# A short setup for a token tower: counts from two 16-way one-hots, and attention logits in unsplit f32 by quarters of the array

## The reference

```
h = take(weight.T, x)                       # 64 x 128 tokens, 64 features
n = layernorm(h)
q, k, v = n @ Wq, n @ Wk, n @ Wv            # 8 heads of 64
a = sigmoid(8 * einsum('bifh,bjfh->bijh', q, k))
h = h + relu(einsum('bijh,bjfh->bifh', a, v) @ Wo)
n = layernorm(h)
h = h + sum over the two best of 6 experts of gate * mlp3(n)
```

## Time and profile before

| | us |
|---|---|
| median of 3 runs | 335.9 |
| lowest, highest | 335.36, 340.27 |
| the profiled execution | 338.1 |
| its span, first to last instruction | 336.3 |
| start of the first unit (end of the setup) | 63.05 |

### The profile page before, as it was taken

One profiled execution on the slowest core, in us unless ns is written; L12 is line 12 of the kernel. 1 busy time (PEld: TensorE's weight loads), 2 busy tenths in 40 slices (PEclk: granted clock), 3 DMA queues, 4 the chain that ended last, 5 costly groups with the idle time before them and its releaser, 6 DMA issues.

```text
span 336.3 us, 4648 instructions
## 1 busy us (share of the span) xinstructions
PE 241.6 (72%) x1636; PEld 130.7 (39%) x1636; DVE 211.6 (63%) x493; ACT 129.1 (38%) x242; POOL 140.4 (42%) x180
## 2 busy tenths in 40 slices
PE   0797663556699699880853457297979899898984
PEld 0555563555556276440323445131424243232221
DVE  4336799756457567452164766867888877946432
ACT  1125437335455355340111402424453455454540
POOL 3000224188987978975021274271536240410110
PEclk9999977585779789996795755877999799999999
DMA  8218300047777667667000003782475556848741
GB/s 173 41 52 122 79 2 0 0 129 206 202 207 193 176 184 204 176 179 219 0 0 2 1 2 77 158 175 59 88 178 135 132 111 128 189 99 179 175 91 31
DMA packets 32263, 38.28 MB, mean 114 GB/s; under 512 B 21936, under 2 KB 23024, under 8 KB 32240
## 3 DMA queue, kind: packets, MB, share of 16 engines
q1 hardware_dynamic: 20240, 20.36, 28.0%
q0 software_dynamic: 10336, 17.05, 18.7%
q10 hardware_dynamic: 1664, 0.58, 0.8%
HBM read 18.30 MB, written 2.83 MB: 63 GB/s over the span
## 4 chain that ended last, share of the span: by engine, by line
PE 37%; DVE 23%; POOL 13%; DMA 12%; issue 6%; ACT 6%; SPq 2%; ACTq 0%; POOLq 0%; DVEq 0%
POOL G L231 12%; DMA G<-Gs 7%; PE PS L688 6%; PE PS L813 5%; PE PS L784 5%; PE PS L800 4%; PE PS L726 4%; DVE OHt L884 3%; PE PS L670 3%; ACT H L502 3%; DVE lead L1076 2%; DVE ex L1078 2%; DMA xb<-ids_scratch 2%; DMA wo_s<-wo 2%; DVE AH L926 2%
## 5 line engine op out<-in xcount | busy, mean ns | idle before, releaser
L231 POOL DMA_DIRECT2D G<-Gs x128 | 76.4, 605 | 19.1 <-DVE Gs L993 10.4
L670 PE MATMUL PS<-AH,BD 128*128 128x256 f32 x256 | 41.0, 326 | 19.5 <-ACT Gs L487 9.9
L688 PE MATMUL PS<-G,cnt 128*64 128x512 f32 x128 | 36.2, 692 | 15.4 <-DMA G<-Gs 15.4
L670 PEld LDWEIGHTS PS<-AH,BD 128*128 128x128 f32 x256 | 38.6, 231 | 22.1 <-DVE BD L946 11.3
L1055 DVE SCALAR_TENSOR_TENSOR H2g<-PS,nb_s,WB 128x1024 f32<-128x1024 f32 x24 | 30.7, 1280 | 14.7 <-PE PS L800 14.7
L993 DVE COPY Gs<-PS 128x512 f32<-128x512 f32 x32 | 21.1, 687 | 28.2 <-DMA G<-Gs 24.8
L502 ACT ACTIVATE H<-PS,b_s 128x512 f32<-128x512 f32 x48 | 30.3, 681 | 19.4 <-PE PS L784 19.4
L800 PE MATMUL PS<-H,W2s 64*64 64x512 f32 x192 | 27.9, 653 | 8.3 <-ACT H L502 8.2
L487 ACT ACTIVATE Gs<-PS 128x512 f32<-128x512 f32 x32 | 18.0, 596 | 40.9 <-DMA G<-Gs 32.6
L961 DVE SCALAR_TENSOR_TENSOR Htab<-PS,table 128x128 f32<-128x128 f32 x64 | 16.8, 382 | 22.8 <-PE PS L699 22.7
L784 PE MATMUL PS<-X,W1s 64*128 64x512 f32 x96 | 29.4, 692 | 0.7 <-ACT H L502 0.7
(11 more groups left out here) (117 smaller groups left out, 405.2 us busy)
## 6 DMA issues: line engine op xcount, KB each, us to landing
G<-Gs POOLq DMA_DIRECT2D x128, 128.0 KB, 3.7
WB<-gate_scratch SPq DMA_DIRECT2D x16, 768.0 KB, 8.8
xb<-ids_scratch SPq DMA_DIRECT2D x8, 256.0 KB, 6.5
h_out<-Y SPq DMA_DIRECT2D x8, 256.0 KB, 6.8
VOr<-vo_scratch SPq DMA_DIRECT2D x2, 512.0 KB, 7.0
GG<-gate_scratch SPq DMA_DIRECT2D x64, 12.0 KB
vo_scratch<-VOs SPq DMA_DIRECT2D x1, 512.0 KB, 3.9
cst<-consts SPq DMA_DIRECT2D x1, 313.0 KB, 4.6
```

The source lines that it names most:

```text
L231: eng.dma_start(G2[half % G2_RING][first:first + 4 * (CG - 1) + 1:4, :, :], Gs[n % GS_RING][:, m, :]).then_inc(done[n % GS_RING], 16)
L670: ins = pe.matmul(o, BD[n % BD_RING][:, part, gl].rearrange("p c f -> p (c f)"), AH[:, r * UG + gl, :], start=(part == 0), stop=(part == 1))
L688: ins = pe.matmul(PS[u * NB:(u + 1) * NB, B_O + m % 2, :], cnt[:, k, :], G2[(2 * fg + k) % G2_RING][:, f:f + 2, :].rearrange("p f a -> p ( ...
```

## The change

The setup is written anew; the stages of the table and the tokens keep their instructions and their order.

- **Counts.** The eight bits of an id are parted into two sets of four (masks 0x4E and 0xB1). DVE masks the ids twice and compares each against 16 constants for all 64 rows at once (`OHa`, `OHb`: 128 x 1024 each). 64 matmuls of 16 x 16 give the counts, after logits step 1. DVE copies them to `cnt_l` after step 5, and two DMAs on SyncE's queue (SP) bring them to `cnt`'s layout.
- **Logits.** `TS` holds unsplit f32, 64 columns to a group, the same in both halves of the partitions; ACT copies banks 0 and 2, DVE banks 1 and 3. `NDhi` and `NDlo` are gone. A step is eight f32 matmuls on quarters of the array.
- **Order.** PE transposes the table ahead of the `WVO` products; `VOp` is cut after steps 0 and 2.

```diff
-VO_AT = 3
-OH_EARLY = 8
-OB = 4
+VO_AT = 0
+NC = 16
+BH = NB // 2
...
-        TS = sb("TS", [P, NG, 2, CG, HEADS], F32R, setup)
-        OHt = sb("OHt", [P, 2, OB, NV], BF16, setup)
+        TS = sb("TS", [P, NG, CG, HEADS], F32, setup)
+        xa, xc_ = sb("xa", [P, NB], I32, setup), sb("xc_", [P, NB], I32, setup)
+        OHa, OHb = sb("OHa", [P, NB, NC], BF16, setup), sb("OHb", [P, NB, NC], BF16, setup)
+        cnt_l = sb("cnt_l", [D, NC, BH], F32, setup)
...
@@ send_unit, and contract(0) alike
-                eng.wait_ge(cnt_sb, 1)
+                eng.wait_ge(cnt_ld, 32)
...
@@ sync, ahead of the first two x_load
+            sp.wait_ge(cnt_sb, 2)
+            for u in range(2):
+                sp.dma_start(cnt[:, :, u * BH:(u + 1) * BH],
+                             cnt_l[32 * u:32 * u + NC].rearrange("a (n k) b -> a n k b", k=VK)).then_inc(cnt_ld, 16)
...
@@ scalar
-            for b in range(4):
+            for b in (0, 2):
                 act.wait_ge(t_ps, b + 1)
-                act.activation(head_pair(TS[:, :, 0], b),
+                act.activation(head_pair(TS[:], b),
...
@@ tensor
+            def counts():
+
+                pe.wait_ge(oh_ready, 2)
+                for b in range(BH):
+                    for u in range(2):
+                        ins = pe.matmul(PS[32 * u:32 * u + NC, 5, b * NC:(b + 1) * NC], OHa[:, u * BH + b, :],
+                                        OHb[:, u * BH + b, :], start=True, stop=True)
+                ins.then_inc(cnt_ps, 1)
...
-            pe.wait_ge(nd_lo, 1)
-            pe.wait_ge(t_dup, 2)
+            pe.wait_ge(t_act, 2)
+            pe.wait_ge(t_dve, 2)
             for t in range(8):
                 if t >= 2:
                     pe.wait_ge(as_ready, t - 1)
-                for j in range(4):
-                    o = PS[:, 2 * (t % 2) + j // 2, (j % 2) * NV:(j % 2 + 1) * NV]
-                    w = TS[:, 4 * t + j].rearrange("p u c h -> p (u c h)")
-                    pe.matmul(o, w, NDhi[:], start=True, stop=False)
-                    ins = pe.matmul(o, w, NDlo[:], start=False, stop=True)
+                for j in (0, 2, 1, 3):
+                    rows = slice(D * (j // 2), D * (j // 2) + D)
+                    for v in range(2):
+                        ins = pe.matmul(PS[v * D:(v + 1) * D, 2 * (t % 2) + j // 2, (j % 2) * NV:(j % 2 + 1) * NV],
+                                        TS[rows, 4 * t + j].rearrange("p c h -> p (c h)"), nT[rows, :],
+                                        start=True, stop=True, skip_group_check=True)
                 ins.then_inc(lg_ps, 1)
-                if t >= 2:
-                    for a in one_hots_with(t - 2):
-                        count(a)
+                if t == 1:
+                    counts()
...
@@ vector
+            dve.tensor_scalar(xa[:], xt_i[:], A_BITS, None, ALU.bitwise_and).then_inc(x_bits, 1)
+            dve.tensor_scalar(xc_[:], xt_i[:], B_BITS, None, ALU.bitwise_and).then_inc(x_bits, 1)
+            for n, (oh, bits, at) in enumerate(((OHa, xa, C_CA), (OHb, xc_, C_CB))):
+                dve.wait_ge(x_bits, n + 1)
+                dve.tensor_tensor(oh[:], bits[:].unsqueeze(2).broadcast_to([P, NB, NC]),
+                                  cst[:, at:at + NC].unsqueeze(1).broadcast_to([P, NB, NC]), ALU.is_equal)\
+                   .then_inc(oh_ready, 1)
...
+            for b in (1, 3):
+                dve.wait_ge(t_ps, b + 1)
+                dve.tensor_copy(head_pair(TS[:], b),
+                                PS[:, T_BANKS[b], :].rearrange("p (h g c) -> p h g c", h=2, c=CG)).then_inc(t_dve, 1)
```

More of the change, by code:

```diff
@@ L64 @@
 H_RING = 5
-C_ID, C_IOTA, C_MASK, C_SEL, C_BM, C_TIE, C_ROW, C_END = 0, 128, 130, 138, 138 + 192, 334, 370, 370 + 256
+C_ID, C_IOTA, C_MASK, C_SEL, C_BM, C_TIE, C_CA, C_CB, C_END = (
+    0, 128, 130, 138, 138 + 192, 334, 370, 370 + NC, 370 + 2 * NC)
+A_BITS, B_BITS = 0x4E, 0xB1
 def home(r, m):
@@ L177, in build @@
         ld_r, ld_w1, ld_b, ld_w2, ld_w3 = (sem(n) for n in ("ld_r", "ld_w1", "ld_b", "ld_w2", "ld_w3"))
-        ln0, ln0_pool, const_ready, nT_ps, nT_sb, nd_hi, nd_lo, x_f = (sem(n) for n in (
-            "ln0", "ln0_pool", "const_ready", "nT_ps", "nT_sb", "nd_hi", "nd_lo", "x_f"))
+        ln0, ln0_pool, const_ready, nT_ps, nT_sb, x_bits = (sem(n) for n in (
+            "ln0", "ln0_pool", "const_ready", "nT_ps", "nT_sb", "x_bits"))
         ld_ids, ids_ok, ids_st = sem("ld_ids"), sem("ids_ok"), sem("ids_st")
-        k_ps, k_sb, t_ps, t_hi, t_lo, t_dup = (sem(n) for n in ("k_ps", "k_sb", "t_ps", "t_hi", "t_lo", "t_dup"))
+        k_ps, k_sb, t_ps, t_act, t_dve = (sem(n) for n in ("k_ps", "k_sb", "t_ps", "t_act", "t_dve"))
         wvo_ps, wvo_sb, vo_ps, vo_sb, vo_st, vo_ld, vo_hi, vo_ready = (sem(n) for n in (
             "wvo_ps", "wvo_sb", "vo_ps", "vo_sb", "vo_st", "vo_ld", "vo_hi", "vo_ready"))
-        oh_ready, cnt_ps, cnt_sb = sem("oh_ready"), sem("cnt_ps"), sem("cnt_sb")
+        oh_ready, cnt_ps, cnt_sb, cnt_ld = sem("oh_ready"), sem("cnt_ps"), sem("cnt_sb"), sem("cnt_ld")
         lg_ps, as_ready, ah_hi, ah_dve, ah_pool = (sem(n) for n in ("lg_ps", "as_ready", "ah_hi", "ah_dve", "ah_pool"))
@@ L424, in _ @@
             act.dma_start(W3s[:], w3.rearrange("(q p) o -> p q o", p=P)).then_inc(ld_w3, 16)
+            act.wait_ge(nT_ps, 1)
+            act.activation(nT[:], PS[:, 6, 0:NV], ACT.Copy).then_inc(nT_sb, 1)
             act.wait_ge(wvo_ps, 1)
@@ L574, in _ @@
         def _(pe):
+            pe.wait_ge(ld_c, 16)
+            pe.wait_ge(ln0, 6)
+            for k in range(VK):
+                ins = pe.transpose(PS[:, 6, k * P:(k + 1) * P], nn0[:, k].rearrange("p u d -> p (u d)"), ident)
+            ins.then_inc(nT_ps, 1)
             pe.wait_ge(ld_v, 16)
@@ L582, in _ @@
             ins.then_inc(wvo_ps, 1)
[L583 to L603, removed]
             pe.wait_ge(ld_k, 16)
@@ L611, in _ @@
                     ins.then_inc(k_ps, 1)
-                    count(2 + q // 2)
+            pe.wait_ge(wvo_sb, 2)
             for k in range(VK):
@@ L617, in _ @@
                   .then_inc(vo_ps, 1)
-                count(4 + k)
             pe.wait_ge(ld_q, 16)
@@ L627, in _ @@
                     ins.then_inc(t_ps, 1)
-            for a in range(OH_EARLY - 2, OH_EARLY):
-                count(a)
+            def counts():
[5 more added lines that the diff above has]
+                ins.then_inc(cnt_ps, 1)
             pe.wait_ge(sel_dve, 1)
@@ L677, in contract @@
                 if m == 0:
-                    pe.wait_ge(cnt_sb, 1)
+                    pe.wait_ge(cnt_ld, 32)
                     pe.wait_ge(bias_dve, 1)
@@ L895, in _ @@
                                   ALU.mult).then_inc(ln0, 1)
[L896 to L901, removed]
             dve.wait_ge(ld_b, 48)
@@ L927, in _ @@
                                       ALU.subtract).then_inc(ah_dve, 1)
-                for a in one_hots_with(t):
-                    one_hots(a)
+                if t == 5:
+                    dve.wait_ge(cnt_ps, 1)
+                    for u in range(2):
+                        dve.tensor_copy(cnt_l[32 * u:32 * u + NC],
+                                        PS[32 * u:32 * u + NC, 5, :].rearrange("a (b n) -> a n b", n=NC))\
+                           .then_inc(cnt_sb, 1)
                 if t == VO_AT:
@@ L932, in _ @@
                     dve.tensor_copy(VOp[:, 0], VOr[:]).then_inc(vo_hi, 1)
-                if t == VO_AT + 1:
+                if t == VO_AT + 2:
                     dve.wait_ge(vo_hi, 1)
                     dve.tensor_tensor(VOp[:, 1], VOr[:], VOp[:, 0].bitcast(F32), ALU.subtract).then_inc(vo_ready, 1)
-            dve.wait_ge(cnt_ps, NB // OB)
-            dve.tensor_copy(cnt[:].rearrange("p k b -> p (k b)"), PS[:, 5, 0:VK * NB]).then_inc(cnt_sb, 1)
             def bd(n):
@@ L1182, in shape_constants @@
                 for i in range(CG):
-                    c[:, C_ROW + k * P + home(r, m) + 4 * i] = k * P + (r * UG + m) * CG + i
+                    at, token = home(r, m) + 4 * i, k * P + (r * UG + m) * CG + i
+                    c[:, C_CA + at // 8] = token & A_BITS
+                    c[:, C_CB + at % 8 * VK + k] = token & B_BITS
     return c
```

14 lines of the change are left out of this document (2 added, 12 removed).

## The result

The changed kernel takes **322.25 us** (median of 4, 321.4 to 323.14); the kernel before, run again beside it, 337.38 (335.36 to 340.27). The ratio is 0.955, 95% interval 0.946 to 0.963: faster by 4.5%, 15.1 us. The profiled execution took 322.91, its span is 321.1. Every ratio and interval here leaves out slow executions, those over 1.5% above the fastest of the same kernel, while a median in us is that of all executions.

The account below looks back on a forecast made before the run. DVE's one-hots, then the cut of `VOp`, were taken to bound the setup's logits; 6.0 us gained ahead of the logits and 6.7 in them make 12.7, so 335.9 - 12.7 = 323.2 us, range 317 to 329.

Parts of the forecast that it names:

- DVE's one-hots as the bound: Logits steps before the change: DVE, busy 5.27 of 5.30 us with one-hots, sets the pace from step 1 on.
- Start: Setup's beginning: two masks and two comparisons take 2.82 us for 2.09; smaller constants table could give 1.68, taken as 0.
- Products: Ahead of the logits: keys gain 2.1 us, dropped count groups 1.2; first logits at 26.2 for 32.20.
- The quarters: Logits step of eight quarter matmuls: 2.0 us for 1.7; rival without overlap 8.2 a step, 370 us, chance 0.03.
- Counts: 64 matmuls of 16 x 16 between logits steps 1 and 2: 2.4 us, upper bound 6.3.
- The loop of the steps: From first logits to first unit: 24.1 us, with POOL held by DVE's early `VOp` cut; first unit at 50.3.
- Costed at nothing: Setup's transfers: `VOr` lands by about 32.5, `cnt` has 5 us of slack, loads of ids land before the first send.
- Behind the first unit: From the table's first unit to the end: nothing changes, 273 us as before.
- The rival of the rising clock: Dense products bring PE to 2.4 GHz: products shrink some 6 us, logits 3.7; 22.4 less, 313.5 us; chance 0.08.
- its milder form: Only the logits phase runs at full clock: 319.5 us, inside the forecast range.

Follow-up runs that it names:

- the late cut: The changed kernel with `VOp` cut after steps 3 and 5 rather than 0 and 2; ratio 0.970 to the kernel before, first unit 49.76.
- the second trace: The changed kernel, unaltered, run and profiled again beside others on one chip; 322.05 us, ratio 0.965 to the kernel before, first unit 50.27.

## Why the prediction was right

The forecast was 323.2 (317 to 329) with the first unit at 50.3; measured are 322.25 and 49.62. The main mechanism is the one forecast: DVE's one-hots held the logits, and without them the first unit starts 13.4 us earlier for 12.7. That the number came out this close is in part luck. The first logits came 2.1 us too early and the stretch behind them was 1.4 too long. And the sum took 12.7 from a median of 335.9; the kernel before then read 337.38 in the series of the result and 333.96 in the last one, so the gain itself was 15.1 and 11.9, on either side of the 12.7. Step by step:

- **DVE's one-hots as the bound**: right. Taken out with the order, under the old logits, they bring 11.4 us; kept, under the new logits, 2.4 are left. The window of 5.10 us in the earlier trace rows was misread as step 0: by its 24 records, eight a step, it holds steps 0 to 2, so DVE set PE's pace from step 3 on, not from step 1. The sum does not use it.
- **Start**: priced right (comparisons 1.22 each, twice), and the transposes at 8.23 for 9.2, since the table of constants landed 0.87 earlier in this execution (0.48 in the second). I took 0 of a bound of 1.68; how much of it is the table's size is not settled.
- **Products**: the order gained, by its undoing, 0.8 us at the keys. The keys ran at 0.93 us a matmul of 256 columns for 1.02 in the earlier trace rows, and all products took 12.5 us for the 13.6 priced. First logits at 24.09 for 26.2: the earlier start of the keys (1.1) and the pace (1.2) explain the 2.1, less 0.2 for a longer way from the last product to the logits.
- **The quarters**: 1.85 a step for 2.0, and the overlap needs both halves of the rows.
- **Counts**: mis-sized. I took 2.4 us; they took 0.97, under the 38 ns each of the row that I priced them by. The rule from the Trainium skill, TensorEngine Tiling (Array Packing), Instruction Overhead, that I set beside it was further off: 50 ns, with 15 measured, and no drain shows around them, the next row following within 0.1 us.
- **The loop of the steps**: 25.5 us from first logits to first unit for 24.1, two errors against each other. PE was faster than priced (counts, and full pace for steps 2 to 5), so step 3 was not late. But the waits between DVE and POOL were under-counted. I had POOL held once, 1.1 us by L911, and DVE once, at step 6's cast. In the trace POOL is held twice (3.24 and 4.05 for 2.35), and four rows of DVE are lengthened: three casts (2.84, 2.83 and 1.91 for 0.69) and one that I did not look for. `BD` is excluded too, 3.51 for 1.42, because POOL's last subtraction (46.52 to 48.90) falls on it. In the earlier trace rows that subtraction held L926 and `BD` came after it, which hid this.
- **Costed at nothing**: `cnt` right, its two DMAs, issued from 42.87 on, landed 2.2 us after their issue, some 9 before the first send at 54.75; the loads of ids at 44.19 with 5.9 to landing were out of the way too. `VOr` landed at 29.82 rather than 32.5 and DVE waited 0.70 for it; harmless, as the late cut shows.
- **Behind the first unit** the prediction had no change, "273 us"; it took 271.5 for 273.3. The 1.8 us come behind the fourth lookup, and no run shows a cause in the change. They count towards the measured gain and not towards the mechanism.

The rival of the rising clock did not come in the products, where most of its price lay; its milder form, the logits alone at full clock, came for steps 2 to 5. The window rows of the changed kernel (window, length, PE busy, clock, DMA share, GB/s):

```profile
8.20:24.00 15.80, 15.43 (x52) 1.00 0.25 72
...
28.60:30.60 2.00, 1.97 (x40) 1.00 0.03 3
30.90:32.00 1.10, 1.08 (x16) 1.00 0.00 0
36.40:38.50 2.10, 1.99 (x16) 0.50 0.03 8
```

A step takes 1.09 at 30.92 with a granted clock of 1.00 and 1.99 at 36.45 with 0.50, so those are 2.4 and 1.2 GHz. The column falls to 0.50 between 35.2 and 35.6, after PE had stood idle from 32.0 to 34.45. The products of the first row have the pace of the lower level although their clock reads 1.00 as well: before the first fall the column is no witness here, the durations are. PE had been busy 15.43 of 15.80 us and stayed slow; the Trainium skill's rule in TensorE: Matmul & The Clock Gate, What's actually happening, that sustained activity opens the gate, is not borne out by f32 products of this kind.

Nor is it the counts that raise the pace, though in this trace it is up only behind them. In the second trace of the same kernel it rose within steps 0 and 1, ahead of them:

```profile
24.50 3.11 PE L637 MATMUL PS<-nT,TS 64*64 64x256 f32 x32 [0.44 <-DVE TS L889]
27.54 0.96 PE L618 MATMUL PS<-OHb,OHa 128*16 128x16 bf16 x64
```

The same two steps took 2.95 to 3.55 in five other kernels, one of them (2.95) with the old counts. With one row half the pace stayed low in front of the counts and behind them. What raises it these runs leave open.

For the exclusion the Trainium skill, SBUF — State Buffer, Who interferes with whom, has the rule that fits every row above: a port pair is shared by VectorE and GpSimd; VectorE contends for it when it reads two SBUF inputs while GpSimd reads SBUF too, or when it runs a copy, cast or tensor_scalar in a two-port mode, and whoever issues second waits to the end. It names `BD`'s kind of instruction, which my sum had left out; in what mode `BD` runs no row shows, only that it waited.

## What to carry to other kernels

When the bound of a stage is taken off, price the next loop with the engines' mutual waits in it, and for every operation that the other engine can exclude, not for those alone that showed a wait before. An operation that runs beside another engine's can be cheaper on the busy engine: 4.9 us more work on DVE gave 1.8 us back at the first unit, though the times alone do not tell the two kernels apart. Quarters of the array want both halves of the rows: with one, a step took 3.5 us for 1.85.

## What was not expected of the hardware

- Count matmuls of 16 x 16 in two column groups by turns ran at 15 ns each (64 in 0.96 to 0.97 us in all twelve traces that have them).
- Quarter products of f32, 256 columns, cost 1.85 us for eight at the lower clock whether the row halves alternate or not (3.75 for two steps against 3.69), and 3.5 with one row half only.
- About 19 us of nearly unbroken f32 matmuls (8.23 to 27.7) went by at the lower pace. It rose ahead of the counts in some traces and behind them in others, and with one row half not before the first unit.
